# Query products of the second layer's attention: per batch inside the loop, or for four batches at once ahead of it

## Chip, cores and metric

One NeuronCore of a Trainium2 chip runs the whole program. The metric is the time of one execution on the device in microseconds (us), the median of several runs; smaller is better.

## The reference

Eight batches (B = 8) of 100 tokens (S) with 256 features (D) go through two transformer layers: attention and a mixture of experts, then latent attention and a gated network with 8-bit rounding. The change touches only the second layer's attention, which computes, for 16 heads:

```python
q_hk = (hidden_q @ Wq.T).reshape(Bv, Sv, H, K)
q_big = jnp.einsum('bshk,hkq->bshq', q_hk, w_kc_q)          # 192 features a head
q_big = _apply_rope(q_big, sin_q[...], cos_q[...])          # rotation by position
kv_r = _apply_rope(kv_c, sin_k[None], cos_k[None])          # 1444 keys of 64 features
q_r = jnp.einsum('bshq,hqr->bhsr', q_big, W_qr)
k_r = jnp.einsum('bld,hdr->bhlr', kv_r, W_kr)
scores = jnp.einsum('bhsr,bhlr->bhsl', q_r, k_r)
attn = jax.nn.softmax(scores, axis=-1)
ctx_c = jnp.einsum('bhsl,bld->bhsd', attn, kv_r)
```

`hidden_q` is the normalised output of the first layer, so no query can be made before the experts of the first layer have finished for that batch. The kernel has folded the weights beforehand: `wqb` and `wqt` hold Wq times w_kc_q (the first 128 and the last 64 of the 192 features of every head), `amat` holds W_qr times W_kr, so that a head's query ends as 64 "latent" numbers which meet the rotated keys directly.

## The kernel before

**Stages.** The first layer's attention and the folding of weights fill the first 140 us of the trace, the shared expert and the routed experts run until about 255 us. Then comes a stretch that this text calls the front (255.3 to 306.1 us), and then the loop over the second layer (306.1 to about 880 us), and a short end.

**The loop.** It runs over 8 batches with 48 slots each, or over 16 units `u` (half a batch: 8 heads, 24 slots; units 2b and 2b+1 are batch b). One slot is one `scores` (two products of a key tile with 400 query columns, a main part `qh` with `khl` and a remainder part `ql` with `kh1`, L1197) and one exponential on ACT (L1674) into one of eight buffers `pt`. Each slot from 1 to 21 of a unit also has one `max_chunk` of the next unit (L1177, 482 keys), reduced on DVE (`reduce_max`, L1976): the row maxima have to be known before the unit's own scores. After slots 7, 15 and 23 stand the `values` products of four tile pairs (L1209), so a unit has three phases of eight slots. POOL adds the exponentials up (`add_weights`, L614) and rotates the keys of the batch after next (L594 to L597). Between these, at fixed slots, stand the transposes of the next keys (`turn_keys`, L1158), the output product (L1232) and the gated network of the batch before. All engines work through orders that are written out by hand; they meet at semaphores only.

**The queries.** For unit u + 2, the loop of unit u makes: `q_big` (L1116 and L1121) with 100 columns (one batch's tokens) against the weights of each head, in the slots QB_AT = 1, 3, 5 of the first two phases; `rope` on DVE (L1943, L1947), which multiplies by cosine and sine into `xyz`; `q_latent` (L1143), after slot 23, ahead of the third values products; `keep_q` on ACT (L1592), which rounds to the fast 32-bit form `qh`; and `low_q` on DVE (L1957), which puts the rounding remainder into `ql`. Units 14 and 15 have no such work, since no unit u + 2 is left. The queries of units 0 and 1 are made in the front.

**The front.** The PE transposes batch 0's keys, makes the eight `shared_out` products of the first layer (L1008), transposes the normalised input `xn3` of batch 0 and 1 (`turn_x3`, L1098), the q work of units 0 and 1, all 21 maximum chunks of unit 0, and six transposes of the gated network's weights (`turn_ternary`, L1085). DVE finishes the first layer's output per batch (`second_residual` L1918, `third_input` L1923 to L1927) and normalises it (`norm_x3`, L1933); POOL fetches the experts' rows (`xn<-ys_scratch`, L689) and does the inverse roots (L636).

A float32 product of one tile is two passes in the trace, each an instruction of its own; a product in the fast form (`qh`, `ql`, `khl`) is one. The SP engine issues nearly all transfers in one hand-written order; `place_max` (L512) moves the row maxima into the last row of `ql`, and the first scores of a unit wait for it.

## Time and profile before

| what | value |
|---|---|
| median of 3 runs | 905.37 us (898.53 to 906.08) |
| span of the profiled execution, first to last instruction | 903.0 us (the page gives no other time for it) |
| busy share PE, DVE, ACT, POOL | 92%, 65%, 44%, 50% |
| front, 255.3 to 306.1 us: PE busy | 41.95 of 50.8 us |
| a middle unit pair, units 12 and 13 | 37.1 and 35.8 us |

The span is the sum that stages are taken from; the median of the runs lies 2.4 us above it. Busy shares are averages over stages: PE is busy for 36.21 of the 37.1 us of unit 12, and less in the front. "PEclk" is the clock that TensorE was granted: 1.00 is 2.4 GHz, 0.50 is 1.2 GHz.

### The profile page before, as it was taken

The numbers are of one execution on the slowest core, as the hardware profiler recorded it, in microseconds if no ns is written. First come the engines' busy times: TensorE is split into PE (matmuls) and PEld (weight loads), VectorE is DVE, ScalarE is ACT, GpSimd is POOL, SyncE is SP. The second block draws the span as 40 slices with busy tenths as digits, with TensorE's granted clock in tenths as the row PEclk, the third lists the DMA queues.
The fourth block names the chain that finished last, engine by engine and source line by source line (L and its number), as shares of the span: only waits on it lengthen the run. The fifth ranks groups of instructions, "written<-read, shape, count | busy, mean of one in ns | idle before, by whom it ended". The sixth has DMA issues, their size and how long they took to land.

```text
span 903.0 us, 15604 instructions
## 1 busy us (share of the span) xinstructions
PE 826.4 (92%) x5844; PEld 606.6 (67%) x5844; DVE 585.3 (65%) x1133; ACT 397.2 (44%) x883; POOL 453.2 (50%) x465
## 2 busy tenths in 40 slices
PE   4998879999998799999999999999999999999883
PEld 3566656788887667677667677676767766765442
DVE  3437864213358675677878778778787787786545
ACT  2248852222231454544544454454354454444441
POOL 3000002800041187768776876776776776567630
PEclk9979996999999899999999999999999999999986
DMA  9532022789810100000000100000000000000000
GB/s 212 187 123 89 2 67 79 261 299 317 299 46 10 35 1 12 18 10 10 19 10 1 31 10 2 10 26 7 10 23 10 10 6 10 2 16 10 2 13 11
DMA packets 42168, 52.28 MB, mean 58 GB/s; under 512 B 12230, under 2 KB 35704, under 8 KB 41836
## 3 DMA queue, kind: packets, MB, share of 16 engines
q1 hardware_dynamic: 41068, 49.63, 17.5%
q0 software_dynamic: 1024, 1.64, 0.6%
q8 instruction: 47, 0.77, 0.3%
q14 instruction: 29, 0.24, 0.1%
HBM read 45.80 MB, written 5.36 MB: 57 GB/s over the span
## 4 chain that ended last, share of the span: by engine, by line
PE 68%; DVE 13%; ACT 7%; DMA 5%; issue 5%; SPq 1%; POOL 0%; POOLq 0%; ACTq 0%; DVEq 0%
PE ps L1197 14%; PE ps L1209 10%; PE ps L1177 7%; PE ps L1116 6%; PE ps L1121 3%; PE ps L1232 3%; DMA xs<-xs_scratch 3%; PE ps L1042 3%; PE ps L994 3%; PE ps L1143 3%; ACT sm L1465 2%; PE ps L1055 2%; DVE xyz L1947 2%; DVE xyz L1943 1%; PE ps L893 1%
## 5 line engine op out<-in xcount | busy, mean ns | idle before, releaser
L614 POOL TENSOR_TENSOR acc<-acc,pt 120x800 f32<-120x800 f32 (+1 forms) x157 | 299.1, 1905 | 94.4 <-ACT pt L1674 61.4
L1674 ACT ACTIVATE pt<-ps 120x400 f32<-120x400 f32 (+1 forms) x384 | 190.1, 505 | 222.5 <-PE ps L1197 211.6
L1976 DVE TENSOR_REDUCE nm<-ps 128x1 f32<-128x482 f32 (+1 forms) x336 | 213.7, 655 | 100.3 <-PE ps L1177 98.1
L1197 PE MATMUL ps<-qh,khl 128*120 128x400 f32 (+1 forms) x384 | 157.9, 411 | 11.1 <-ACT pt L1674 8.3
L1209 PE MATMUL ps<-pt,kv 120*64 120x400 f32 (+1 forms) x768 | 143.8, 510 | 0.0
L1177 PE MATMUL ps<-khl,qh 128*128 128x482 f32 (+1 forms) x336 | 131.6, 393 | 5.3 <-DVE nm L1976 4.6
L1197 PE MATMUL ps<-ql,kh 65*120 65x400 f32 (+1 forms) x384 | 134.3, 350 | 0.0
L1197 PEld LDWEIGHTS ps<-qh,khl 128*120 128x120 f32 (+1 forms) x384 | 70.9, 185 | 58.6 <-issue 32.4
L1209 PEld LDWEIGHTS ps<-pt,kv 120*64 120x64 f32 (+1 forms) x768 | 51.9, 138 | 65.8 <-issue 55.8
L636 POOL TENSOR_TENSOR rstd<-veps,mhalf 100x1 f32<-100x1 f32 (+2 forms) x20 | 13.4, 670 | 158.1 <-DVE veps L1808 114.6
L1197 PEld LDWEIGHTS ps<-ql,kh 65*120 65x120 f32 (+1 forms) x384 | 71.3, 186 | 5.1
L1116 PEld LDWEIGHTS ps<-x3T,wqb 128*128 128x128 f32 x512 | 68.3, 195 | 3.1 <-issue 0.7
L614 POOL TENSOR_TENSOR acc<-pt,pt 121x800 f32<-121x800 f32 x16 | 30.6, 1910 | 77.0 <-ACT pt L1674 77.0
L1177 PEld LDWEIGHTS ps<-khl,qh 128*128 128x128 f32 (+1 forms) x336 | 60.1, 179 | 12.6 <-DVE nm L1976 8.9
L1116 PE MATMUL ps<-x3T,wqb 128*128 128x100 f32 x512 | 67.3, 275 | 0.7 <-ACT x3T L1429 0.5
L1042 PE MATMUL ps<-xsT,egu 128*128 128x128 f32 x448 | 52.6, 276 | 1.0 <-DVE hs L1900 0.6
L1042 PEld LDWEIGHTS ps<-xsT,egu 128*128 128x128 f32 x448 | 51.9, 192 | 1.8 <-ACT xsT L1429 1.3
L1592 ACT ACTIVATE qh<-ps 64x400 fp32r<-64x400 f32 x64 | 31.9, 499 | 46.6 <-PE ps L1143 46.1
L689 POOL DMA_INDIRECT xn<-ys_scratch,slot x8 | 8.5, 1067 | 78.2 <-DMA ys_scratch<-ysb 76.2
L1947 DVE TENSOR_TENSOR xyz<-ps,ropeq 64x200 f32<-64x200 f32 x128 | 46.2, 361 | 1.3
L1908 DVE TENSOR_TENSOR hT<-sg,ps 128x512 f32<-128x512 f32 x14 | 9.6, 686 | 48.2 <-PE ps L1042 48.2
L1232 PE MATMUL ps<-bmat,ct 128*100 128x256 f32 x128 | 33.5, 385 | 6.4 <-DVE ct L1997 5.8
(277 smaller groups left out, 1246.0 us busy)
## 6 DMA issues: line engine op xcount, KB each, us to landing
egu<-_L_ffn_gate_up_proj_dram SPq DMA_DIRECT2D x14, 1024.0 KB, 6.0
edn<-in_L_ffn_down_proj_dram SPq DMA_DIRECT2D x14, 512.0 KB, 7.1
spread<-inv_scratch SPq DMA_DIRECT2D x30, 100.0 KB, 2.7
craw<-in_ctx_dram SPq DMA_DIRECT2D x8, 360.0 KB
wo_n<-in_L_xattn_Wo_dram SPq DMA_DIRECT2D x1, 2048.0 KB, 10.5
wq_n<-in_L_xattn_Wq_dram SPq DMA_DIRECT2D x1, 2048.0 KB, 8.0
xs_scratch<-zero SPq DMA_DIRECT2D x1, 1792.0 KB, 9.9
xs<-xs_scratch SPq DMA_DIRECT2D x14, 128.0 KB, 6.1
```

What stands on the lines that cost most here:

```text
L614: nc.gpsimd.tensor_tensor(total[r, :, :], before[r, :, :], pt[j % PT_BUF][r, :, :], ALU.add).then_inc(p_added, 1)
L994: last = mm(ps[:, 2 * (k % 2) + a, 0:HT], sgu[:, c, a, 128 * m:128 * m + 128], xnT[:, c, HT * n:HT * n + HT], start=c == 0, stop=c == DC - 1)
L1042: last = mm(ps[:, 2 * (t % 2) + a, TR * m:TR * m + TR], egu[t % EBUF][:, c, FI * a + 128 * m:FI * a + 128 * m + 128], xsT[t % 2][:, c, :], ...
L1116: mm(ps[:, q_bank(u, a), S * part:S * part + S], wqb[:, c, h, 0:128], x3T[:, c, :], start=c == 0, stop=c == DC - 1)
L1177: mm(ps[0:w, 3 + m % 2, 0:MN], qh[u % 2][:, 128 * i:128 * i + w], khl[b % 2][:, MSTART[n]:MSTART[n] + MN], start=True, stop=True).then_inc ...
L1197: last = mm(ps[0:key_rows(t), k % 2, 0:HT], lhs[:, keys], rhs[:, HT * a:HT * a + HT], start=first, stop=not first)
L1209: last = mm(ps[CD * a:CD * a + CD, 2, 0:HT], kv[b % KV_BUF][r, t, :], pt[j % PT_BUF][r, a, :], start=t == 0, stop=t == KT - 1)
L1232: last = mm(ps[0:S, 6, 0:D], ct[:, S * i:S * i + S], bmat[:, i, :], start=i == 0, stop=i == GH - 1)
L1592: last = nc.scalar.activation(qh[u % 2][p:p + CD, HT * a:HT * a + HT], ps[CD * a:CD * a + CD, 5, 0:HT], ACT.Copy)
L1674: nc.scalar.activation(pt[j % PT_BUF][0:rows, k % 2, :], ps[0:rows, k % 2, 0:HT], ACT.Exp).then_inc(p_ready, 1)
L1947: last = tt(o[CD * j:CD * j + CD, 2, e:HG:2, :], ps[CD * e:CD * e + CD, bank + 1, 0:HT // 2].rearrange("p (i q) -> p i q", i=HG // 2), rop ...
L1976: nc.vector.tensor_reduce(nm3[0:w, i, n:n + 1], ps[0:w, 3 + m % 2, 0:MN], AX.X, ALU.max).then_inc(m_reduced, 1)
```

## The change

All queries are made before the loop, and no longer for one batch but for four batches side by side, so that the columns of a product grow from 100 to 400 (HT). The work is cut into eight quads `n`: `quad(n)` gives the half of the batches g, the half of the heads p and a pair of heads e; a quad makes four heads of four batches. Per quad:

- PE: `q_tail` twice (the last 64 features of two heads, 2 products), `q_main` four times (one head's first 128 features, 2 products), and `q_latent` of the quad before (12 products of 400 columns), which stands behind the two tails.
- DVE: four `rope`s of two multiplications each (was: six per `rope`), two `low_q`. ACT: four pairs of copies of tails into `tail2` (`keep_tail`) and two `keep_q`. POOL: four multiplications of tails by the rotation table (`rope_tail`).
- SP: `store_q`, four transfers of 64 x 4 x 200 numbers (205 KB each) into the DRAM tensor `q_scratch`.

For each unit of the loop `load_q` brings the queries back with three transfers of 64 x 800 numbers (205 KB each); `qh` and `ql` get a third buffer (QBUF = 3). The maximum chunks of unit 0 stand in quads 4, 5 and 6 (MAX_IN), the six weight transposes in quads 0, 2 and 3, the transposes of the inputs of batches 4 to 7 in quads 1 and 2. The loop loses `q_big`, `rope`, `q_latent`, `keep_q`, `low_q`, `turn_x3` and `norm_x3`; some waits that went with them change. Units 14 and 15 keep their instructions.

```diff
+HB = B // 2
+QUADS = 2 * NU // HB
+QBUF = 3
+MAIN_BANK, TAIL_BANK, LATENT_BANK = (0, 1), (6, 7), (2, 5)
+TERNARY_IN, X3_IN, MAX_IN = (0, 0, 2, 2, 3, 3), (1, 1, 2, 2), (4, 5, 6)
...
+        def store_q(sp, n):
+
+            g, p, e = quad(n)
+            sp.wait_ge(q_hi, 2 * n + 2)
+            sp.wait_ge(q_lo, 2 * n + 2)
+            heads = q_dram.rearrange("(g b p) l d (a e n) -> g p l a e d b n", g=2, b=HB, p=PAIRS, a=2, e=2)
+            for l, src in enumerate((qhi[e], qlo[e])):
+                for a in range(2):
+                    sp.dma_start(heads[g, p, l, a, e],
+                                 src[CD * a:CD * a + CD, :, :, :].rearrange("d b i s -> d b (i s)").bitcast(F32)).then_inc(q_stored[e], 16)
+
+        def load_q(sp, u):
+
+            n = 2 * PAIRS * (u // PAIRS // HB) + 2 * (u % PAIRS)
+            for e in range(2):
+                sp.wait_ge(q_stored[e], 64 * (n // 2 + 1))
+            if u == QBUF - 1:
+                sp.wait_ge(latent_done, 2 * QUADS)
+            elif u >= QBUF:
+                sp.wait_ge(s_done, LANE * (u - QBUF + 1))
...
-            place_max(sp, 0)
+            for n in range(4):
+                store_q(sp, n)
+            load_q(sp, 0)
+            load_q(sp, 1)
...
+            store_q(sp, 4)
+            store_q(sp, 5)
+            place_max(sp, 0)
+            store_q(sp, 6)
+            store_q(sp, 7)
             for u in range(NU):
                 b = u // PAIRS
+                if u + 2 < NU:
+                    load_q(sp, u + 2)
...
+            for e in range(2):
+                pool.wait_ge(q_stored[e], 64 * QUADS // 2)
             pool.wait_ge(fq_turned, 6)
...
+            def q_main(n, a, i):
+
+                g, p, e = quad(n)
+                m = 4 * n + 2 * a + i
+                if m >= 2:
+                    pe.wait_ge(rope_done, m - 1)
+                h = 2 * HG * p + HG * a + 2 * e + i
+                for c in range(DC):
+                    last = mm(ps[:, MAIN_BANK[i], 0:HT], wqb[:, c, h, 0:128], x3T[:, c, HT * g:HT * g + HT],
+                              start=c == 0, stop=c == DC - 1)
+                last.then_inc(main_done, 1)
...
                 if c == 0:
-                    pe.wait_ge(q_hi, u + 1)
+                    pe.wait_ge(ld_q[u % QBUF], 48 * (u // QBUF + 1))
...
+            for n in range(QUADS):
+                q_tail(n, 0)
+                q_tail(n, 1)
+                if n:
+                    q_latent(n - 1)
+                for a in range(2):
+                    for i in range(2):
+                        q_main(n, a, i)
+                        if n in MAX_IN:
+                            for c in range(MC):
+                                if c // 7 == MAX_IN.index(n) and c % 7 // 2 == 2 * a + i:
+                                    max_chunk(0, c)
...
-                    if u + 2 < NU and f < 2 and x in QB_AT:
-                        for part in range(2):
-                            q_big(u + 2, f, 2 * QB_AT.index(x) + part)
...
+            def rope(n, a, i):
+
+                m = 4 * n + 2 * a + i
+                dve.wait_ge(main_done, m + 1)
+                if n:
+                    dve.wait_ge(latent_done, 2 * n)
                 for j in range(2):
+                    last = tt(xy[a][i][:, j, :].rearrange("p (b q) -> p b q", b=HB),
+                              ps[:, MAIN_BANK[i], 0:HT].rearrange("p (b q) -> p b q", b=HB),
+                              ropeq[:, j, :].unsqueeze(1).to_broadcast([128, HB, S]), ALU.mult)
                 last.then_inc(rope_done, 1)
```

PE of the kernel before, in a first phase of unit 0 in the loop (x3T is the transposed input, wqb and wqt are the query weights, qh with khl is a score or a maximum chunk):

```order
516 L1197 MATMUL ps<-ql_198,kh_188 120x400
517 L1177 MATMUL ps<-khl_187,qh_197 128x482 [waits m_reduced]
518 L1158 MATMUL ps<-ident,kv_104 64x120 [waits k_kept,kv_ready]
519 L1158 MATMUL ps<-ident,kv_104 64x120 x3
520 L1197 MATMUL ps<-qh_196,khl_187 120x400 [waits p_ready]
521 L1197 MATMUL ps<-ql_198,kh_188 120x400
522 L1177 MATMUL ps<-khl_187,qh_197 128x482 [waits m_reduced]
523 L1116 MATMUL ps<-x3T,wqb 128x100 x4
524 L1197 MATMUL ps<-qh_196,khl_187 120x400 [waits p_ready]
```

PE of the changed kernel at the same place, in the first phase of the loop:

```order
611 L1283 MATMUL ps<-qh_202,khl_193 121x400 [waits p_ready]
612 L1283 MATMUL ps<-ql_203,kh_194 121x400
613 L1263 MATMUL ps<-khl_193,qh_204 128x482 [waits m_reduced]
614 L1242 MATMUL ps<-ident,kv_104 64x121 [waits q_lo,kv_ready]
615 L1242 MATMUL ps<-ident,kv_104 64x121 x3
616 L1283 MATMUL ps<-qh_202,khl_193 121x400 [waits p_ready]
617 L1283 MATMUL ps<-ql_203,kh_194 121x400
618 L1263 MATMUL ps<-khl_193,qh_204 128x482 [waits m_reduced]
```

Between the maximum chunk and the next score nothing of the queries is left.

PE of the changed kernel in quad 4, ahead of the loop (zt are rotated tails, xy rotated main features):

```order
492 L1226 MATMUL ps<-zt_232,amat 64x400
493 L1226 MATMUL ps<-zt_237,amat 64x400
494 L1209 MATMUL ps<-x3T,wqb 128x400 [waits rope_done]
495 L1209 MATMUL ps<-x3T,wqb 128x400
496 L1263 MATMUL ps<-khl_193,qh_202 128x482 [waits fq_kept,k_kept,ld_q0]
497 L1263 MATMUL ps<-khl_193,qh_202 128x482 [waits fq_kept]
498 L1209 MATMUL ps<-x3T,wqb 128x400 [waits rope_done]
499 L1209 MATMUL ps<-x3T,wqb 128x400
500 L1263 MATMUL ps<-khl_193,qh_202 128x482 [waits m_reduced] x2
```

The latent products of quad 3 end at 493; the first maximum chunk of unit 0 stands one head's main product behind them, and now waits for a transfer (ld_q0).

SP of the changed kernel at that time:

```order
150 L555 DMA q_scratch<-qhi_130 64x4x200 [waits q_lo,q_hi]
151 L555 DMA q_scratch<-qhi_130 64x4x200
152 L555 DMA q_scratch<-qlo_131 64x4x200 x2
153 L568 DMA qh_202<-q_scratch 64x800 [waits q_stored1,q_stored0]
154 L568 DMA qh_202<-q_scratch 64x800
155 L569 DMA ql_203<-q_scratch 64x800
```

The load of unit 0's queries stands behind the four stores of quad 3, which wait for the remainders (q_lo) of quad 3's latent products.

SP of the kernel before, at the end of the front:

```order
140 L468 DMA ys_scratch<-ysb_163 128x256 [waits ys_kept]
141 L512 DMA ql_198<-nmr_194 1x6x128 [waits m_kept]
142 L512 DMA ql_198<-nmr_194 1x16x2
143 L568 DMA lnw_b<-in_L_ffn_ln_weight_dram 100x1024 [waits fq_turned]
144 L480 DMA craw_105<-in_ctx_dram 120x768 [waits kv_ready]
```

Nothing stood between the experts' last store and the row maxima; now 32 stores and six loads do.

## Rows read from the trace of the kernel before

**Rows 1.** The page: busy time by engine, and the clock in 40 slices.
```profile
PE 826.4 (92%) x5844; PEld 606.6 (67%) x5844; DVE 585.3 (65%) x1133; ACT 397.2 (44%) x883; POOL 453.2 (50%) x465
...
PEclk9979996999999899999999999999999999999986
```
**Rows 2.** Busy time by stretch: front, cold start, units 0, 1, 12, 13, 14.
```profile
core 0: us, PE busy (x) PEld busy (x) DVE busy (x) ACT busy (x) POOL busy (x), PEclk, DMA share, GB/s
255.30:306.10 50.80, 41.95 (x344) 32.98 (x343) 36.53 (x83) 15.63 (x26) 12.41 (x13) 1.00 0.08 23
306.10:312.00 5.90, 5.87 (x21) 5.61 (x21) 2.84 (x7) 1.85 (x4) 0.00 (x0) 0.50 0.41 124
306.10:342.20 36.10, 35.38 (x226) 26.24 (x226) 24.43 (x50) 17.29 (x35) 25.84 (x23) 0.91 0.07 21
342.20:373.70 31.50, 31.48 (x223) 22.99 (x221) 20.52 (x40) 15.27 (x32) 24.90 (x22) 1.00 0.06 20
738.10:775.20 37.10, 36.21 (x249) 26.73 (x247) 28.74 (x62) 18.89 (x39) 22.07 (x15) 1.00 0.02 7
775.20:811.00 35.80, 35.05 (x247) 24.79 (x245) 27.62 (x47) 16.77 (x34) 21.48 (x12) 1.00 0.04 10
811.00:841.50 30.50, 28.93 (x141) 17.59 (x139) 21.09 (x43) 13.86 (x29) 19.67 (x12) 1.00 0.03 8
```
**Rows 3.** PE in order of time, unit 12: start, us, engine, line, operation.
```profile
739.19 1.03 PE L1116 MATMUL ps<-x3T,wqb 128*128 128x100 f32 x8
740.00 0.42 PE L1197 MATMUL ps<-qh,khl 128*121 128x400 f32 x1
...
742.73 0.58 PE L1158 MATMUL ps<-ident,kv 121*64 121x121 f32 x4
743.08 0.42 PE L1197 MATMUL ps<-qh,khl 128*121 128x400 f32 x1
```
**Rows 4.** PE in order of time, end of unit 12.
```profile
770.28 2.28 PE L1143 MATMUL ps<-xyz,amat 128*64 128x100 f32 x48
772.39 2.86 PE L1209 MATMUL ps<-pt,kv 120*64 120x400 f32 x16
775.18 0.45 PE L1197 MATMUL ps<-qh,khl 128*121 128x400 f32 x1
```
**Rows 5.** Groups by line: name, forms, count, busy us, mean ns, idle before.
```profile
L614 POOL TENSOR_TENSOR acc<-acc,pt 120x800 f32<-120x800 f32 (+1 forms) x157 | 299.1, 1905 | 94.4 <-ACT pt L1674 61.4 <-issue 17.0 <-POOL kv L597 8.6
L1976 DVE TENSOR_REDUCE nm<-ps 128x1 f32<-128x482 f32 (+1 forms) x336 | 213.7, 655 | 100.3 <-PE ps L1177 98.1
L1943 DVE TENSOR_TENSOR xyz<-ps,ropeq 128x400 f32<-128x400 f32 x64 | 33.4, 562 | 0.9 <-PE ps L1121 0.7
L1592 ACT ACTIVATE qh<-ps 64x400 fp32r<-64x400 f32 x64 | 31.9, 499 | 46.6 <-PE ps L1143 46.1
```
**Rows 6.** DVE in order of time, from unit 12 into unit 13.
```profile
769.94 0.41 DVE L2001 TENSOR_TENSOR x_sb<-x_sb,ps 100x256 f32<-100x256 f32 x1
...
776.47 1.15 DVE L1957 TENSOR_TENSOR ql<-ps,qh 64x400 fp32r<-64x400 f32 x2
```
**Rows 7.** Busy time of a stretch of the shared expert: PE only has 400-column passes.
```profile
156.00:169.50 13.50, 13.50 (x41) 7.60 (x40) 2.86 (x5) 2.59 (x6) 11.59 (x25) 1.00 0.98 356
```
**Rows 8.** PE in order of time, front.
```profile
271.18 1.89 PE L1008 MATMUL ps<-sdn,hs 128*100 128x256 f32 x8
```
**Rows 9.** SP's issues in order of time, unit 2.
```profile
384.91 1.18 SPq L489 DMA_DIRECT2D inv<-sums  x2
387.58 0.33 SPq L492 DMA_DIRECT2D inv_scratch<-inv  x1
388.94 1.13 SPq L499 DMA_DIRECT2D spread<-inv_scratch  x2
```
**Rows 10.** The page: DMA issues, KB each, us from issue to landing.
```profile
spread<-inv_scratch SPq DMA_DIRECT2D x30, 100.0 KB, 2.7
...
ys_scratch<-ysb SPq DMA_DIRECT2D x14, 128.0 KB, 6.1
```
**Rows 11.** PE in order of time, start of the loop.
```profile
306.13 0.66 PE L1197 MATMUL ps<-qh,khl 128*121 128x400 f32 x1 [2.34 <-DMA ql<-nmr]
```

More of the change, by code:

```diff
@@ L270, in build @@
         assert cursor[0] <= after_qb
+        cursor[0] = after_keys
+        xn3 = [place(f"xn3_{i}", [S, D]) for i in range(2)]
+        qhi = [place("qhi0", [128, HB, 2, S], F32R)]
+        qlo = [place("qlo0", [128, HB, 2, S], F32R)]
+        assert cursor[0] <= after_qb
+        cursor[0] = after_qb
+        qhi += [place("qhi1", [128, HB, 2, S], F32R)]
+        qlo += [place("qlo1", [128, HB, 2, S], F32R)]
+        assert cursor[0] <= after_fw
         cursor[0] = after_qb
@@ L1652, in _ @@
                 keep_keys(0, j)
[L1653 to L1662 removed]
+            for b in range(HB):
+                keep_x3(b)
+            for n in range(QUADS):
+                keep_tail(n, 0)
+                keep_tail(n, 1)
+                if n:
+                    keep_q(n - 1, 0)
+                    keep_q(n - 1, 1)
+                for t in range(6):
+                    if TERNARY_IN[t] == n and n < 2:
+                        keep_ternary(t)
+                for b in range(HB, B):
+                    if X3_IN[b - HB] == n:
+                        keep_x3(b)
+                for t in range(6):
+                    if TERNARY_IN[t] == n and n >= 2:
+                        keep_ternary(t)
+                if n == MAX_IN[-1]:
+                    keep_max(0)
+            keep_q(QUADS - 1, 0)
+            keep_q(QUADS - 1, 1)
             for b in range(B):
@@ L1696, in _ @@
                         keep_max(u + 1)
-                    if u + 2 < NU and at == LANE - 1:
-                        keep_q(u + 2)
             def last_silu(half):
@@ L1952, in low_q @@
-            def low_q(u):
-                dve.wait_ge(q_hi, u + 1)
-                for a in range(2):
-                    cols = slice(HT * a, HT * a + HT)
-                    last = tt(ql[u % 2][0:CD, cols], ps[CD * a:CD * a + CD, 5, 0:HT],
-                              qh[u % 2][CD * a:CD * a + CD, cols].bitcast(F32), ALU.subtract)
-                last.then_inc(q_lo, 1)
+                dve.wait_ge(rstd_ready, AFTER_3 + b + 1)
+                if b >= 2:
+                    dve.wait_ge(x3_turned, b - 1)
```

401 lines of the change are left out of this document (194 added, 207 removed).

## The prediction

> **What bounds the kernel now.** I read the page first [rows 1]: PE is busy for 92% of the span, at 2.4 GHz in nearly every slice, and no other engine for more than 65%. That is an average, so the stages come next, as stretches [rows 2]. In the loop, unit 12 lasts 37.1 us with PE busy for 36.21, unit 13 lasts 35.8 with 35.05: PE sets the pace, and DVE (28.74), POOL and ACT have room. In the front PE works 41.95 of 50.8 us. The first 5.9 us of the loop run at half clock. The most telling row is unit 14: it has no query work (no unit 16 follows), lasts 30.5 us, and PE stands idle for 1.6 of them. So query work costs time in the loop, and without it PE is no longer quite alone at the limit. Then I read single pieces in order of time, for what one piece costs on PE from the start of one instruction to the start of the next; "busy" and mean durations would overstate it, as passes overlap.
>
> **What the loop loses.** Eight passes of q_big take 0.81 us (739.19 to 740.00) [rows 3]; a unit has six such pieces: 4.9. The 48 passes of q_latent take 2.1 us (770.28 to 772.39) [rows 4]. Together 7.0 us a unit, for the 14 units 0 to 13.
>
> Not all of it comes back, because what was beside it has lost its cover:
> - Even units. Unit 14 is the template: 30.5 us [rows 2]. It lacks three key transposes, 0.35 us each (742.73 to 743.08) [rows 3], which the others keep. With them and a little for ACT's copies of the keys I take 31.9 us, against 37.1: 5.2 won of 7.0. The missing part is pacing: with no q_big between them, slots follow each other at PE's 0.6 us, but each has a reduction of 0.655 us on DVE [rows 5], and each maximum chunk waits for the second last reduction.
> - Odd units. From 769.94 to 776.47 DVE is occupied with the residual, the normalisation and the rounding of the batch before [rows 6]; the values products (775.18 less 772.39, 2.8 us) and the latent products (2.1 us) have covered that [rows 4]. Now 2.1 us of cover go, the third maximum chunk of the next unit waits, and I count 1.2 us of the 7.0 as given back: 5.8 won.
> - Six pairs (units 2 to 13): 6 x 11.0 = 66 us.
> - Units 0 and 1 [rows 2]: 36.1 less 7.0, less 2.9 for the half-clock start (5.9 us of work at half rate), which I expect to vanish, as PE comes out of dense products; and 31.5 less 7.0. Plus 0.5 for pacing that makes 51.2. POOL, however, needs 11 additions of 1.905 us [rows 5] and some 6 us of key rotation a unit, 27 us, 54 for two, and begins only when quad 7's stores have landed, about 7 us into the loop. The sums of unit 1 are wanted some 7.5 us into unit 2, so PE waits about 3 us: 54. From 67.6: 13 won.
>
> Loop: 79 us won. The ends are 101 us (14 x 7.0 + 2.9, nothing given back) and 70 us (a further 0.7 us lost a unit).
>
> **What the front gains.** First the price of a 400-column pass: in a stretch of the shared expert with nothing else on PE, 40 to 41 passes start in 13.5 us [rows 7], 0.336 us each. The latent products write half the output columns each and run in pairs as the values products do: 16 passes of 400 columns in 2.8 us (772.39 to 775.18) [rows 4], 0.174 each. So a quad has 2 tails of 4 passes (2.7 us), 4 mains of 4 passes (5.4) and 24 latent passes (4.2): 12.3 us, and eight quads 98 us. All 16 units of the old way cost 16 x 7.0 = 112 us. Larger products save PE just 14 us, since a 100-column pass is already cheap in place (0.10 us) and four times the columns cost 3.3 times that. Everything else about this change is where the time lies and what waits.
>
> A rule points elsewhere. The Trainium skill, "TensorE: Matmul & The Clock Gate", section "Back-to-back issue gap", gives N / 2.4 + 2.5 ns for an isolated product at full clock, 0.169 us for 400 columns; the row of float32 passes shows twice that [rows 7]. By that rule of the Trainium skill the quads' 288 pass times would take 49 us instead of 97, and the sum would come out 48 us lower.
>
> The front in order:
> 1. Until the first tail product. The four remaining shared_out products (1.89 us each [rows 8]) alternate on DVE with residual, normalisation and PE's transpose, some 3.4 us a round from 265: first tail at 278.7 us. POOL has two memsets ahead of the first rotation, so `rope` starts near 284.
> 2. Quad 0 without latent products, with two weight transposes: done at 289. Within a quad DVE does not delay PE: a rope is two multiplications of 0.56 us [rows 5], 1.1 against 1.34 for a main product. ACT's tail copies (0.5 us each [rows 5], 8 a quad) and POOL's four multiplications (between a half and one addition of 800 columns [rows 5], at most 7.6 us a quad) also fit into 12.3.
> 3. Quads 1 to 3 with four input and four weight transposes: 3 x 12.3 + 4 = 41: 330.
> 4. Quad 4: tails and the latent products of quad 3 end at 337. Now the first maximum chunk of unit 0 is one main product (1.3 us) away, and its load stands on SP behind the four stores of quad 3, which wait for ACT and DVE to split quad 3's latent products (about 1.4 us). SP spends 0.59 us on an issue (1.18 for two, 1.13 for two) [rows 9]; seven issues are 4.1, and a load of 100 KB lands 2.7 us after its issue [rows 10]. The last of the three loads is issued 5 us after the latent end and lands at about 8, so PE stands for some 7 us. What hides it otherwise is nothing: the chunk blocks every product behind it. Bounds: 4 us (issues at half price) and 14 (a store of 128 KB needs 6.1 us under load [rows 10], and the loads queue behind 820 KB).
> 5. Behind a pause of 2.34 us PE ran 5.9 us at half clock at the start of the loop [rows 2, 11]. After 7 us I expect the same, 2.4 us lost. Bounds: 0 and 3.
> 6. Quads 4 to 6 carry seven reductions of 0.655 us each beside four ropes of 1.1 (9.0 us of DVE [rows 5]) against 6.8 us of PE in the same stretch; part of it runs on under the tails. 1.4 us lost a quad, and 2.5 behind quad 6, where the transpose of the maxima waits for the last reduction. Quad 7 ends with 1.4 us of wait for its last rope, since no tails follow.
>
> Sum: 337 + 1.3 + 6.8 (stall) + 2.4 (half clock) + 6.9 (three mains, seven chunks at 0.2 us, 1.4 of DVE) = 354.4 for quad 4; quads 5 and 6 15.1 each (12.3 + 1.4 + 1.4), and 2.7 behind them; quad 7 12.3, and its last wait and latent products 5.6: the loop starts at about 405 instead of 306 us, 99 us later. Bounds: 85 (no stall, no DVE pacing) and 112.
>
> The Trainium skill, "DMA: Bandwidth & Descriptors", section "Anatomy of one DMA", gives 2.0 us plus bytes over 436 GB/s. That rule makes the seven transfers (1.43 MB) 5.3 us, and the stall would shrink only if SP's issue time were nil.
>
> **The sum.** 903.0 + 99 - 79 = 923 us against the profiled span. The three runs reach from 4.5 below the span to 3.1 above it, so the median gives no firm offset, and I take 922.
>
> **Rivals.**
> - *The loop gives everything back (ends faster).* Its place is slots 24 to 31 and 0 to 7 of the loop. If DVE's chains are not the limit there, each unit wins 7.0: 101 us, less POOL's 3. With the front at 99 that is 904; if the load also arrives in time (9 less), it is 895, and with the DVE wait behind quad 6 gone too, 893. It counts as faster from 7.0 a unit on. For it: PE is 97% busy and DVE 77% in unit 12 [rows 2]. Against it: unit 14, where PE idles for 1.6 us with less to do. Time 893 to 904.
> - *The load is in time, the loop paced as I say.* If stores and load overlap PE fully, 9 us less: 914. For it speaks that units 0's and 1's queries are long stored by then; against it SP's order.
> - *Transfers bind every quad.* A quad stores 820 KB in four issues. `keep_q` needs the stores of two quads ago, so it decides once the queue moves less than 820 KB in 12.3 us, 67 GB/s. At 55 GB/s (15 us) six quads lose 2.6 each, 16 us: 939. Against it: 356 GB/s moved in one stretch [rows 7].
> - *POOL rules the loop.* With 27 us a unit against 31 it does not; at full pace it would only cap an upside at 27 a unit.
> - *The small products were free and the loop loses nothing.* Then 1000 us; unit 14 excludes it.
>
> **Chances.** A measurement of this kernel can tell about 1% (9 us) from no change. Forecast with its own spread 0.62 (909 to 933), of which some 0.10 falls within 1% of before; load in time 0.14, most of it within 1%; loop gives all back 0.10, half within 1% and half faster; transfers bind 0.13, slower; the rate of the Trainium skill's page on TensorE 0.01, 874 us, faster. That is faster 0.06, within 1% 0.27, slower 0.67. The range 904 to 938 takes in the late-transfer case nearly whole and the in-time case, and leaves the fastest out.
>
> **What would show it.** Right: the loop starts near 405 us; passes in the quads start 0.336 us apart; one wait of 5 to 9 us at L1263 for the load of qh near 338 us, with half clock behind it; units 2 to 13 at 61 to 63 us a pair; unit 14 unchanged at 30.5. Wrong: quads longer than 13 us with PE waiting at L1226 for DVE, ACT or POOL; no wait at the first maximum chunk; pairs under 60 us (then the loop gave back less than I took) or over 65, with POOL's additions back to back.

## The result: 928.1 us, 2.7% slower

| | before | after |
|---|---|---|
| median | 905.7 us (898.5 to 906.5, 4 runs) | 928.1 us (924.3 to 933.7, 4 runs) |
| ratio | 1 | 1.0267, 95% interval 1.0211 to 1.0324 |
| profiled execution: span | 903.0 | 931.8 (its time was 933.7) |
| first keys transposed (end of the first layer) | 255.5 | 263.1 |
| front, from there to the first score of the loop | 50.6 | 148.1 (+97.5) |
| first score of the loop to the end | 596.9 | 520.6 (-76.3) |

I had predicted 922 (904 to 938), a front longer by 99 and a loop shorter by 79. The 7.6 us by which the first keys come later lie in code that the change doesn't touch. Over all traces of this study, of both kernels, this point lies anywhere between 252.8 and 263.1 us, about as wide as the run times of one kernel spread (898.5 to 906.5 before, 924.3 to 933.7 after). Hence the sections of the traces, front and loop, are the sharper measure, and I use them beside the ratios: 647.5 us before, 668.7 after. Each is read from a single execution, though. The comparison leaves out runs over 1.5% above the fastest of their kernel; where one run came out very short (888.5 in b_port, 883.7 in a_keys_dve) this bends the ratio of the runs that are left, and there I go by the medians of all runs and by sections.

The page of the changed kernel, busy time and clock, answers to [rows 1]: PE is still the busiest, but its share fell from 92% to 89%.

```profile
PE 830.6 (89%) x4692; PEld 534.7 (57%) x4692; DVE 538.4 (58%) x989; ACT 404.1 (43%) x899; POOL 487.7 (52%) x502
...
PEclk9869997999999998999998999999999999999996
```

The stretches that answer to [rows 2] (us, then busy PE, PEld, DVE, ACT, POOL, granted clock, DMA share, GB/s): front, first 5.9 us of the loop, units 0, 1, 12, 13 and 14.

```profile
263.10:411.20 148.10, 129.99 (x547) 67.58 (x545) 70.70 (x152) 52.91 (x103) 49.11 (x51) 0.97 0.21 57
411.20:417.10 5.90, 5.89 (x33) 4.42 (x33) 4.37 (x7) 4.58 (x10) 0.00 (x0) 1.00 0.51 134
411.20:437.27 26.07, 25.24 (x132) 15.46 (x130) 15.80 (x26) 15.58 (x32) 17.84 (x16) 1.00 0.27 70
437.27:462.28 25.01, 24.73 (x123) 14.53 (x123) 15.11 (x24) 12.98 (x27) 23.47 (x23) 1.00 0.12 33
779.69:810.77 31.08, 29.54 (x152) 18.81 (x150) 23.66 (x45) 16.79 (x35) 21.97 (x17) 1.00 0.09 27
810.77:842.92 32.15, 29.90 (x148) 18.11 (x148) 22.13 (x36) 14.71 (x30) 23.35 (x13) 0.95 0.11 29
842.92:872.21 29.29, 28.44 (x140) 17.62 (x138) 21.14 (x42) 13.85 (x29) 19.67 (x13) 1.00 0.03 8
```

Three things stand out. The loop starts at a granted clock of 1.00 (0.50 before). The even unit 12 is 6.0 us shorter. The odd unit 13, which was shorter than the even one before (35.8 against 37.1), is now longer than it: 32.15 us, PE idle for 2.2 of them, and its clock is 0.95.

The stall in quad 4, PE in order of time:

```profile
343.19 1.61 PE L1209 MATMUL ps<-x3T,wqb 128*128 128x400 f32 x4
353.25 1.17 PE L1263 MATMUL ps<-khl,qh 128*128 128x482 f32 x2 [8.45 <-DMA ql<-q_scratch]
354.22 2.87 PE L1209 MATMUL ps<-x3T,wqb 128*128 128x400 f32 x4
```

and SP's issues beside it:

```profile
344.52 1.23 SPq L555 DMA_DIRECT2D q_scratch<-qhi  x2
345.79 1.33 SPq L555 DMA_DIRECT2D q_scratch<-qlo  x2
347.54 1.16 SPq L568 DMA_DIRECT2D qh<-q_scratch  x2
348.75 0.60 SPq L569 DMA_DIRECT2D ql<-q_scratch  x1
```

Seven issues of some 0.6 us, four stores and three loads, follow the latent products of quad 3; the third load is issued at 348.75 and has landed when PE goes on at 353.25. Behind the wait the same four passes span 2.87 us instead of 1.61, and the granted clock is 0.50 for 4 us:

```profile
353.25:357.20 3.95, 3.95 (x7) 2.49 (x8) 1.30 (x3) 0.00 (x0) 0.00 (x0) 0.50 0.62 164
```

That is the wait that I had placed there, at 8.45 us instead of 6.8.

Where PE waits in the loop, units 0 to 13, changed kernel (us in total, times, longest):

```profile
PE ps L1263 <- DVE nm L2061: 15.4, 12, 2.9
PE ps L1283 <- ACT pt L1769: 8.9, 14, 0.8
PE ps L1304 <- POOL acc L680: 0.6, 1, 0.6
```

The same view of the kernel before:

```profile
PE ps L1232 <- DVE ct L1997: 5.8, 7, 0.8
PE ps L1197 <- ACT pt L1674: 4.0, 7, 0.7
PE ps L1197 <- DMA ql<-nmr: 2.3, 1, 2.3
PE ps L1177 <- DVE nm L1976: 2.1, 5, 0.5
```

The wait for DVE at the maximum chunks has grown sevenfold, and 11.5 of the 15.4 us lie in the first phases of the odd units 3 to 13, one wait in each. These phases last (unit 3, 5, ... 13) 14.7, 12.7, 12.75, 11.4, 11.4, 12.4 us, where the first phase before (11.1 to 12.15) less its three pieces of `q_big` (2.4) would be 8.6 to 9.7.

### The profile page after: what moved, and what is told of

The parts are those of the page before. It is cut to its first block, busy times and chain, and to the rows that moved or that the text cites. A ratio compares the mean times of both kernels' runs of the same rounds, so it can differ in the third digit from the quotient of the medians.

```text
span 931.8 us, 13330 instructions
## 1 busy us (share of the span) xinstructions
PE 830.6 (89%) x4692; PEld 534.7 (57%) x4692; DVE 538.4 (58%) x989; ACT 404.1 (43%) x899; POOL 487.7 (52%) x502
## 4 chain that ended last, share of the span: by engine, by line
PE 59%; DVE 15%; POOL 8%; ACT 7%; DMA 5%; issue 5%; SPq 1%; POOLq 0%; DVEq 0%; ACTq 0%
PE ps L1283 9%; PE ps L1295 8%; POOL acc L680 6%; PE ps L1263 5%; PE ps L1125 4%; PE ps L1209 4%; PE ps L1226 4%; DVE nm L2061 3%; PE ps L1077 3%; DMA xs<-xs_scratch 2%; PE ps L1316 2%; ACT sm L1542 2%; PE ps L1138 2%; PE ps L1197 2%; DVE sg L2129 1%
## 5 line engine op out<-in xcount | busy, mean ns | idle before, releaser
L2061 DVE TENSOR_REDUCE nm<-ps 128x1 f32<-128x482 f32 (+1 forms) x336 | 211.1, 652 | 115.8 <-PE ps L1263 113.8
L1263 PE MATMUL ps<-khl,qh 128*128 128x482 f32 (+1 forms) x336 | 138.1, 414 | 25.5 <-DVE nm L2061 16.1
L702 POOL TENSOR_TENSOR rstd<-veps,mhalf 100x1 f32<-100x1 f32 (+1 forms) x25 | 15.6, 624 | 167.6 <-DVE veps L1899 120.4
L1263 PEld LDWEIGHTS ps<-khl,qh 128*128 128x128 f32 (+1 forms) x336 | 61.7, 184 | 46.8 <-DVE nm L2061 28.8
L775 POOL TENSOR_TENSOR zt<-tail,ropeq 128x400 f32<-128x400 f32 x32 | 33.3, 1045 | 76.9 <-ACT tail L1506 75.9
L1209 PE MATMUL ps<-x3T,wqb 128*128 128x400 f32 x128 | 48.9, 522 | 1.2 <-DVE xy L2033 1.2
L1506 ACT ACTIVATE tail<-ps 64x400 f32<-64x400 f32 x64 | 31.9, 499 | 37.5 <-PE ps L1197 32.8
L680 POOL TENSOR_TENSOR acc<-pt,pt 121x800 f32<-121x800 f32 x16 | 30.7, 1921 | 22.8 <-DMA q_scratch<-qlo 11.2
L2033 DVE TENSOR_TENSOR xy<-ps,ropeq 128x400 f32<-128x400 f32 x64 | 33.7, 568 | 10.7 <-PE ps L1209 8.3
L2043 DVE TENSOR_TENSOR qlo<-ps,qhi 128x400 fp32r<-128x400 f32 x16 | 9.2, 575 | 49.5 <-ACT qhi L1676 49.5
```

What stands on the lines that cost most here:

```text
L680: nc.gpsimd.tensor_tensor(total[r, :, :], before[r, :, :], pt[j % PT_BUF][r, :, :], ALU.add).then_inc(p_added, 1)
L775: nc.gpsimd.tensor_tensor(zt[m % 8][:, :].rearrange("p (b q) -> p b q", b=HB), tail2[i][:, :].rearrange("p (b q) -> p b q", b=HB), ropeq[: ...
L1209: last = mm(ps[:, MAIN_BANK[i], 0:HT], wqb[:, c, h, 0:128], x3T[:, c, HT * g:HT * g + HT], start=c == 0, stop=c == DC - 1)
L1263: mm(ps[0:w, 3 + m % 2, 0:MN], qh[u % QBUF][:, 128 * i:128 * i + w], khl[b % 2][:, MSTART[n]:MSTART[n] + MN], start=True, stop=True).then_ ...
L1506: return nc.scalar.activation(dst, src, ACT.Copy, **more)
L2033: last = tt(xy[a][i][:, j, :].rearrange("p (b q) -> p b q", b=HB), ps[:, MAIN_BANK[i], 0:HT].rearrange("p (b q) -> p b q", b=HB), ropeq[:, ...
```

## The experiments

Two questions: does the stall cost what it seems to, and what holds the odd units? Names with a_ start from the changed kernel, names with b_ from the one before. The sections are read from each trace; the fronts of kernels whose instructions are the same up to there differ by 2.7 us, since the first tail product starts 21.7 us after the first keys in some traces and 24.3 to 24.5 in others; so fronts are compared from the first tail product on.

| run | front | loop to end | sum | ratio to before (95%) |
|---|---|---|---|---|
| before | 50.6 | 596.9 | 647.5 | 1 |
| after | 148.1 | 520.6 | 668.7 | 1.0267 (1.0211 to 1.0324) |
| a_load_early | 140.4 | 520.5 | 660.9 | 1.0141 (1.0086 to 1.0196) |
| b_no_queries | 50.6 | 526.5 | 577.1 | 0.9226 (0.9187 to 0.9266) |
| a_half_adds | 150.5 | 499.8 | 650.3 | 1.0072 (1.0033 to 1.0110) |
| b_half_adds | 50.6 | 592.5 | 643.1 | 0.9980 (0.9928 to 1.0032) |
| a_x4_late | 147.9 | 524.9 | 672.8 | 1.0262 (1.0199 to 1.0326) |
| b_x4_late | 50.6 | 597.6 | 648.2 | 1.0015 (0.9963 to 1.0067) |
| a_spread | 135.4 | 520.3 | 655.7 | 1.0119 (1.0045 to 1.0193) |
| a_best | 138.2 | 523.4 | 661.6 | 1.0202 (1.0130 to 1.0274) |
| a_port | 147.7 | 505.1 | 652.8 | 1.0043 (1.0011 to 1.0076) |
| a_spread_port | 135.4 | 501.9 | 637.3 | 0.9949 (0.9918 to 0.9980) |
| b_port | 50.6 | 593.6 | 644.2 | 0.9873 (0.9817 to 0.9930); medians 900.3 against 902.9 |
| a_keys_dve | 135.4 | 502.7 | 638.1 | 0.9876 (0.9799 to 0.9953); medians 897.5 against 900.9 |

### The load earlier: a_load_early

```diff
-            for n in range(4):
-                store_q(sp, n)
-            load_q(sp, 0)
+            store_q(sp, 0)
+            store_q(sp, 1)
+            load_q(sp, 0)
+            store_q(sp, 2)
+            store_q(sp, 3)
             load_q(sp, 1)
```

> The changed kernel, with the loads of unit 0's and unit 1's queries issued as soon as their quads are stored (load of unit 0 behind the stores of quad 1, load of unit 1 behind those of quad 3). Theory A (SP's order makes the stall, the pause makes the half clock): the wait of 8.45 us at the first maximum chunk goes, and the half-clock stretch behind it too; quad 4, from its first tail to that of quad 5, falls from 25.3 to 14.9 us like quads 5 and 6, and the whole kernel by 10 to 11 us, to 917. Theory B (stores and loads together are too slow for the front, whatever their order): the wait moves or shrinks to 4 us or more, and the kernel gains under 5 us. If only the wait goes and the half clock stays, 8.5.

Theory A. The tails of quads 4 and 5 in this run:

```profile
329.49 2.91 PE L1199 MATMUL ps<-x3T,wqt 128*128 128x400 f32 x8
344.38 2.85 PE L1199 MATMUL ps<-x3T,wqt 128*128 128x400 f32 x8
```

Quad 4, from one row to the other, takes 14.9 us instead of 25.25, so the stall with its slow stretch cost 10.4: 8.45 of waiting and 1.9 of half clock. The ratio to before fell from 1.0267 to 1.0141, some 11 us. It was the order of one queue and not the transfers themselves.

### What the loop can give: b_no_queries

Units 2 to 15 of the kernel before reuse the first two units' queries; nothing is made in their place.

> The kernel before, with the query work of units 2 to 15 left out of the loop on PE, DVE and ACT (q_big, rope, q_latent, keep_q, low_q, and the transposes and normalisations of inputs 2 to 7); these units reuse the queries of units 0 and 1, so the output is not that of the reference. It prices what the loop can give back at most. My prediction's terms: 79 us (70 to 101) gained by the loop; here POOL starts on time, so 82: 905 - 82 = 823. Rival (the loop gives back all 7.0 us a unit): 98 to 101 us, 805. Rival (the odd units' waits in the changed kernel come from missing cover on DVE, not from POOL's late start): units 3, 5, 7 and 9 take 31.5 us or more here too and the gain is 75 or less. If POOL's late start makes them: odd units 30.4 to 31.2 from the beginning.

The loop section is 70.4 us shorter, where I expected 82. Two causes. Its first unit gained only 0.8 us, since the first phase now runs at a granted clock of 0.62 with waits (17.5 us). And the odd units are long without POOL's late start too: unit 3 takes 29.8 us, but units 5 and 9 take 32.35, with 12.6 us in their first phase at a clock of 0.86, like unit 5 of the changed kernel. That is the rival of the missing cover. So POOL's late start cannot be the whole cause; only unit 3 (first phase 9.7 here, 14.7 in the changed kernel) seems to hang on it.

### POOL's additions halved: a_half_adds, b_half_adds

```diff
-            nc.gpsimd.tensor_tensor(total[r, :, :], before[r, :, :], pt[j % PT_BUF][r, :, :], ALU.add).then_inc(p_added, 1)
+            w = 2 if t == 1 else 1
+            nc.gpsimd.tensor_tensor(total[r, 0:w, :], before[r, 0:w, :], pt[j % PT_BUF][r, 0:w, :], ALU.add).then_inc(p_added, 1)
```

> The changed kernel with POOL's additions halved from the second of a unit on (400 of 800 columns a row, 10 of 11 additions), so the sums of half the heads are wrong. Theory P (POOL, which starts 7 us late and has 27 us of work a unit, is behind until unit 5, holds up the inverse root for the rounding chain, and so the maximum chunks of odd units): units 3, 5, 7, 9 fall from 33.5, 33.2, 32.5, 31.1 to about 31, the whole by 5 to 8 us, to 920 to 923. Theory D (DVE's chain itself is too long for the slots): they stay within 0.5 us, and the whole within 2 us of the changed kernel.

> Control: the same halved additions in the kernel before. There POOL idles 2 to 3 us in stretches of a unit, so both theories expect nothing: within 2 us of 905. A gain of more than 3 us would mean that POOL's additions hold the loop up in the kernel before too (or contend with DVE), and then the gain of the halved additions in the changed kernel would say nothing of its late start.

The changed kernel's loop gained 20.8 us, three times what theory P expected, the kernel before 4.4. The 4.4 us are more than the 3 that I had set for the control (by the medians of the runs it is 2.4): the additions cost the kernel before something as well, so the gain is no measure of POOL's late start. Every odd unit fell, those of the middle too. The first phase of unit 5 with whole additions, that of unit 9, and then that of unit 5 with halved ones (us, busy PE, PEld, DVE, ACT, POOL, clock, DMA share, GB/s):

```profile
557.82:570.50 12.68, 10.92 (x53) 6.93 (x54) 7.87 (x13) 5.12 (x12) 11.14 (x13) 0.87 0.17 49
685.66:697.08 11.42, 9.57 (x54) 5.62 (x54) 7.84 (x13) 5.03 (x12) 10.83 (x12) 1.00 0.20 54
```

```profile
545.26:554.95 9.69, 9.56 (x53) 5.62 (x54) 6.14 (x12) 5.01 (x12) 8.17 (x12) 1.00 0.25 64
```

PE's idle 1.8 us are gone, and so is DVE's extra 1.7 us of "busy" time, though DVE's instructions are the same. That was the hint. The two engines side by side at the start of unit 5, changed kernel:

```profile
555.83 0.61 POOL L702 TENSOR_TENSOR rstd<-veps,mhalf 100x1 f32<-100x1 f32 x1 [2.85 <-DVE veps L2090]
556.41 3.94 POOL L680 TENSOR_TENSOR acc<-acc,pt 120x800 f32<-120x800 f32 x2
...
557.24 1.20 DVE L2102 TENSOR_SCALAR xn<-xn,qsc 100x256 f32<-100x256 f32 x1
...
559.11 1.40 DVE L2110 TENSOR_SCALAR xq<-xn 100x256 bf16<-100x256 f32 x1
...
561.99 0.49 PE L1263 MATMUL ps<-khl,qh 128*128 128x482 f32 x1 [1.74 <-DVE nm L2061]
```

POOL waits for the variance; meanwhile the additions of slots 21 and 23 pile up and run back to back from 556.41, one until about 558.4 (half of the 3.94 us) and one until 560.35. DVE's scaling of xn ends at 558.44 and that of xq at 560.51, each within 0.2 us of the end of an addition. With halved additions the same two take 0.354 and 0.484 us in the mean, with whole ones 1.10 and 1.24. DVE stands still while POOL adds; the trace counts it as busy.

The Trainium skill, "SBUF — State Buffer", section "Who interferes with whom", says that VectorE and GpSimd share one pair of ports, which an instruction holds to its end, that `tensor_scalar` can contend for it (in the modes that use both ports), and so do operations with both inputs in SBUF, while `tensor_reduce` on this chip never does. The trace agrees, though no row names the mode in which the scalings run: the maxima take 0.655 us before, 0.652 after and 0.652 with halved additions, but the division `ct<-ctu,spread`, with both inputs in SBUF, shows this in the groups of before, of after and of a_half_adds:

```profile
L1997 DVE TENSOR_TENSOR ct<-ctu,spread 128x400 f32<-128x400 f32 x15 | 9.8, 654 | 2.9 <-DMA spread<-inv_scratch 2.5
```

```profile
L2082 DVE TENSOR_TENSOR ct<-ctu,spread 128x400 f32<-128x400 f32 x15 | 20.1, 1339 | 7.5 <-DMA spread<-inv_scratch 7.3
```

```profile
L2083 DVE TENSOR_TENSOR ct<-ctu,spread 128x400 f32<-128x400 f32 x15 | 9.3, 621 | 6.7 <-DMA spread<-inv_scratch 6.5
```

The change doubled it without touching it, and halved additions take that back: the same instruction now falls where POOL is adding.

### The root later: a_x4_late, b_x4_late

```diff
-    OUT_FROM, RESIDUAL_SLOT, QX_SLOT, X4_SLOT = 17, 21, 23, 19
+    OUT_FROM, RESIDUAL_SLOT, QX_SLOT, X4_SLOT = 17, 21, 23, 23
```

> The changed kernel with POOL's inverse root for the rounding chain placed behind the addition of slot 23 instead of slot 19 (X4_SLOT = 23); nothing else. Theory Q (while POOL waits for the variance, the additions of slots 21 and 23 pile up, and run back to back right behind the root; DVE's two large scalings of the chain, 0.35 and 0.48 us with halved additions, 1.20 and 1.38 with whole ones, stand still until POOL's addition ends): with the additions done ahead of the root both scalings fall to 0.35 to 0.6 us, the first phase of units 5 to 13 from 12.7 or 11.4 to 10 to 11 us, and the whole kernel by 6 to 9 us, to about 0.992 to 0.994 of the changed kernel. Theory R (POOL is simply behind, 27 us of work a unit, and what counts is how late the root comes): the root comes up to 1.9 us later and the kernel gains nothing or loses up to 5 us. Unit 3, where POOL is still behind from its late start, should keep its 14.7 us by both.

> Control: the same X4_SLOT = 23 in the kernel before. There the latent products cover the chain; the halved additions shortened an odd unit by only 0.6 us. Both theories: within 3 us of the kernel before, at most 4 us faster.

Half a miss: theory Q is right on the scalings, theory R on the time. Both scalings fell (0.353 and 0.470 us), but the odd first phases of units 5 to 13 stayed at 11.2 to 13.95 us, that of unit 3 grew to 18.3, and the loop to 524.9. DVE and PE at the start of unit 11:

```profile
743.11 0.21 DVE L2099 TENSOR_SCALAR qsc<-qsc,rstd 100x1 f32<-100x1 f32 x1 [2.04 <-POOL rstd L702]
...
743.81 0.35 DVE L2102 TENSOR_SCALAR xn<-xn,qsc 100x256 f32<-100x256 f32 x1
...
746.34 0.77 PE L1263 MATMUL ps<-khl,qh 128*128 128x482 f32 x1 [1.53 <-DVE nm L2061]
```

The root now comes 2.04 us late, behind the two additions. What the port no longer takes, the queue takes. An edit that takes away both was needed. The control did nothing, as expected.

### The front and POOL's start: a_spread, a_best

a_spread has the early loads, `c * 16 // MC == 4 * (n - 3) + 2 * a + i` for the place of a maximum chunk (quads 3 to 6), the weight transposes in quads 0 and 2, `turn_max(0)` behind the tails of quad 7, and two waits of POOL apart:

```diff
-            for e in range(2):
-                pool.wait_ge(q_stored[e], 64 * QUADS // 2)
+            pool.wait_ge(q_stored[0], 64 * QUADS // 2)
...
+                        if b == 0 and s == ROTATE_SLOT[0]:
+                            pool.wait_ge(q_stored[1], 64 * QUADS // 2)
```

> The changed kernel with three edits ahead of the loop: the early loads of a_load_early; the 21 maximum chunks of unit 0 spread over the 16 main products of quads 3 to 6 instead of 12 of quads 4 to 6, the weight transposes all in quads 0 and 2, and the transpose of the maxima behind the tails of quad 7; and POOL waits for the stores of the even quads only before its first addition, for those of the odd quads before its first key rotation. Against a_load_early: if DVE's seven reductions beside four ropes pace quads 4 to 6 (14.9 us against 12.9 of a quad without chunks), quads 3 to 6 take 13.0 to 13.6 us, the wait for the maxima (1.9 us) goes, and the front is 5 to 7 us shorter, less about 1 us for the moved transposes. POOL starts 4 to 5 us earlier, which takes 2 to 5 us from units 3 and 5. Sum 7 to 11 us: a ratio to the kernel before of 1.002 to 1.006. Rival (PE's own work, not DVE, fills the chunk quads): under 2 us from the front.

> a_spread and X4_SLOT = 23 together. If theory Q holds and the gains add, 6 to 9 us below a_spread: 0.993 to 0.999 of the kernel before. Unit 3 should gain too here, since POOL is less behind when its root comes. If theory R holds, the same as a_spread or slower.

The front: quads 3 to 6 take 14.3, 13.7, 13.7, 13.7 us, the chunk quads of a_load_early 14.9, 14.85, 16.9 (with the wait for the maxima). The moved transposes cost 2.3 in quad 2 and save 0.9 in quad 3, 1.4 where I had said 1. Behind the first tail the front is 113.7 us against 116.0: 2.3 won, not 5 to 7. The earlier start of POOL took 1.0 us from unit 3's first phase (14.7 to 13.7) and nothing measurable from the whole loop (520.3). So quads 3 to 6 gained 3.7 us beside the transposes, 1.9 of it the wait for the maxima; the other 1.8 I put down to DVE's pacing. The transposes take 1.4 of it back. a_best joined it with the late root, and that fails here too: with a ratio of 1.0202 it is slower than a_spread (1.0119), as theory R says.

### Neither queue nor port: a_port, b_port, a_spread_port

```diff
                     if b and s == X4_SLOT:
                         norm_x4(pool, power, b - 1)
+                        if b + 2 < B:
+                            rotate_keys(pool, step, b + 2, 2)
+                        pool.wait_ge(xq_ready, b)
...
-                    if b + 2 < B and s in ROTATE_SLOT:
+                    if b + 2 < B and s in ROTATE_SLOT and not (b and s == 23):
                         rotate_keys(pool, step, b + 2, ROTATE_SLOT.index(s))
```

> The changed kernel with one change of POOL's order for batches 1 to 7: the inverse root stays at slot 19, but behind it come the key rotation of slot 23 (four short multiplications and additions of 0.3 to 0.8 us) and a wait until the rounding chain has written xq, and only then the additions of slots 21 and 23. No work is added or left out. Theory Q (additions that run back to back behind the root hold DVE's two large scalings up, PE then waits 1.7 us, and at three or four units its clock falls): both scalings take under 0.6 us, the first phases of units 5 to 13 fall from 11.4 to 12.75 us to 9.7 to 10.3, PEclk 1.00 in all of them; unit 3 falls by 2 us or more from 14.7 (POOL is still behind there); from the first score to the end 505 to 509 us instead of 520.6, the ratio to the kernel before 1.009 to 1.015. Theory R (POOL's total work is the limit, and time that it stands idle for DVE is added to it): first phases as long as before or longer, or the sums (wait for the last addition) late by 1 to 3 us a unit, 518 to 530 us.

> a_spread with the same order of POOL. Sections of the trace, which leave out how late the first layer ends: front 135.4 us as in a_spread, first score to the end 505 to 508, together 641 to 643, against 647.5 of the kernel before: ratio 0.990 to 0.996. If theory R holds, 1.01 or more, no better than a_spread.

> Control: the same order of POOL in the kernel before. The scalings get shorter there too (1.10 and 1.24 us before), but the latent products cover the chain: the first phases of odd units fall by at most 0.6 us (12.15 to 11.5 or 11.6, as with halved additions), 0 to 4 us in all. If it gains 8 us or more, the additions cost the kernel before as much as the changed one, and the port says nothing about the change.

Theory Q: both scalings are short, every first phase is short at full clock, and the loop takes 505.1 us. It is better than theory Q's own figures in two places, the first phases (9.4 us, where 9.7 to 10.3 was said) and the ratio (1.0043, where 1.009 to 1.015 was said). POOL and DVE at the start of unit 5 in a_port, and its first phase as a stretch:

```profile
543.84 0.61 POOL L702 TENSOR_TENSOR rstd<-veps,mhalf 100x1 f32<-100x1 f32 x1 [2.72 <-DVE veps L2093]
...
546.69 4.29 POOL L680 TENSOR_TENSOR acc<-acc,pt 120x800 f32<-120x800 f32 x2 [0.73 <-DVE xq L2113]
...
545.25 0.35 DVE L2105 TENSOR_SCALAR xn<-xn,qsc 100x256 f32<-100x256 f32 x1
...
546.27 0.28 DVE L2113 TENSOR_SCALAR xq<-xn 100x256 bf16<-100x256 f32 x1
```

```profile
545.72:555.10 9.38, 9.32 (x55) 5.64 (x54) 5.74 (x12) 5.03 (x12) 8.22 (x6) 1.00 0.24 66
```

The first phases of units 5 to 13 take 9.4 us, unit 3's 10.0, all at a clock of 1.00; the odd units 28.8 to 29.95. The loop gained 15.5 us by 0.7 us of idling and an order, with no work less. (The key rotation moved as well; what that does by itself was not measured.) In the kernel before the same order is worth 3.3 us by sections (12.15 to 11.5 us a first phase) and 2.6 by medians: there the latent products had covered what the port takes. The ratio of b_port, 0.9873, would say more, but it hangs on the run of 888.5 us. The three edits of the front and this one together (a_spread_port, 897.8 us against 902.9, ratio 0.9949) beat the kernel before by half a per cent. Against the kernel before with the same order the sections say the same (637.3 against 644.2), but they are one trace each, and the medians, 897.8 and 900.3, are no further apart than such runs scatter; that this version is the faster one is not shown.

### What the even units give back: a_keys_dve

```diff
+                if b:
+                    nc.vector.tensor_copy(khl[b % 2][CD:128, k0:k0 + n], ps[0:CD, 5, 0:n])
                 tt(khl[b % 2][0:CD, k0:k0 + n], ps[0:CD, 5, 0:n], kh1[b % 2][0:CD, k0:k0 + n].bitcast(F32), ALU.subtract)
```

(and ACT's copy into khl left out from batch 1 on)

> a_spread_port, and for batches 1 to 7 one of ACT's two copies of each third of the transposed keys is made by DVE instead (21 copies of 64 x 480 numbers). In a_spread_port PE still waits in the loop 17 times, 10.3 us in all, for ACT's exponentials, in the first two phases of the even units, where ACT has both key copies between its exponentials. Theory K (these copies, not DVE's reductions, are what the even units give back: 31.1 us where 37.0 less 7.0 would be 30.0): the waits for ACT fall below 2 us in all, the even units from 31.1 to 29.9 to 30.3 us, the first score to the end from 501.9 to 493 to 496 us, and the ratio to the kernel before from 0.995 to 0.986 to 0.989. Theory D (my prediction's: the reductions pace the slots, 0.655 us against PE's 0.6): with 0.5 us more on DVE per key tile group the even units stay at 31.1 or grow by up to 0.5 us, and PE's waits move to DVE.

A miss for theory K. Theory D's numbers came true, but not by its mechanism, since the new wait is for a key copy and not for the reductions. An even unit of a_spread_port has two waits; ACT and PE in order of time:

```profile
682.25 1.07 ACT L1735 ACTIVATE hq<-h 100x1024 bf16<-100x1024 f32 x1
...
683.86 0.45 PE L1289 MATMUL ps<-qh,khl 128*121 128x400 f32 x1 [0.54 <-ACT pt L1775]
...
694.33 0.56 ACT L1512 ACTIVATE khl<-ps 64x480 fp32r<-64x480 f32 x1
...
695.47 0.44 PE L1289 MATMUL ps<-qh,khl 128*120 128x400 f32 x1 [0.69 <-ACT pt L1775]
```

The first stands behind ACT's square of the gated network and stayed. The second stood behind the key copies and went, but 0.72 us for DVE at the next key transposes came in its place:

```profile
699.37 0.57 PE L1248 MATMUL ps<-ident,kv 120*64 120x120 f32 x4 [0.72 <-DVE khl L2061]
```

since its copy (0.652 us) now runs in a row with the subtraction. Over the loop PE waits 6.5 us for ACT instead of 11.0, and 5.0 for `khl`. The even units 6 to 12 take 31.2 to 31.3 us, where a_spread_port has 31.0 to 31.1; sections and medians show no difference from a_spread_port. The ratio, 0.9876, lies in theory K's range, but it rests on three runs with the one of 883.7 us among them; the medians make it 0.996.

## Why the prediction was right, and where not

**Right: the sign, the size, and the front.** 928.1 measured, 922 predicted. The front grew by 97.5 instead of 99 us. Its terms: the stall 8.45 (6.8 said), its half clock 1.9 (2.4), DVE's pacing of the chunk quads 0.9 each (1.4; it is 14.85 less 12.55 and my 1.4 for seven chunks), the wait for the maxima 1.9 (2.5), quad 7 with its last rope and latents 18.1 (17.9), quads 1 to 3 with their transposes 40.65 (41). The wait stands where it was said to, and a_load_early showed its cause. It came out longer mainly because the last load took 4.5 us from issue to landing (348.75 to 353.25), where I had taken 2.7 from a smaller transfer. The fit of the Trainium skill, "DMA: Bandwidth & Descriptors", section "Anatomy of one DMA", that I had set beside it says nothing here as I used it: it is given for one transfer, and for those that GpSimd issues, while these seven are issued one after the other by SyncE. That PE gains little by larger products holds: a quad without chunks or transposes is 12.55 us, 0.25 more than my sum. The rate that I had set against it, that of the Trainium skill, "TensorE: Matmul & The Clock Gate", section "Back-to-back issue gap" (0.169 us for 400 columns, an estimate from its formula), is out: the 16 passes of a quad's main products start 0.347 us apart (5.55 us in all).

The closeness of the loop, 76.3 against 79, is luck: the next paragraphs add up errors of 13.9 us one way and 11.1 the other. Nor did all signs come true: of the six pairs of units 2 to 13 two took 61 to 63 us and four 63.2 to 64.4, and unit 14 did not stay at 30.5.

**Wrong: the odd units.** The step is "Odd units ... I count 1.2 us of the 7.0 as given back: 5.8 won". Measured over units 3 to 13 they won 3.5 us each (35.9 to 32.4), so 3.5 us were given back and not 1.2, 13.9 us more than I had said over the six units. The place was right, DVE's chain between 769.94 and 776.47 [rows 6], and so was the thought that it loses its cover; the size was wrong, and the prediction shows no working for it. Most of what is missing lies in the first phases of the odd units: PE stands idle there for 1.5 to 2.9 us each, 1.9 in the mean, and behind the wait the clock fell in four of the six (0.77, 0.87, 0.87, 0.86), which took about 2.8 us in unit 3 and 1.3 in the three others. The prediction had no term for the clock here.

Why the chain is so long I had not seen either. I read 6.5 us of "busy" DVE as work, but 1.7 of them are DVE standing still for POOL's additions, and they did so in the kernel before too:

```profile
771.88 3.92 POOL L614 TENSOR_TENSOR acc<-acc,pt 120x800 f32<-120x800 f32 x2
```

```profile
772.71 1.20 DVE L2017 TENSOR_SCALAR xn<-xn,qsc 100x256 f32<-100x256 f32 x1
...
774.58 1.37 DVE L2025 TENSOR_SCALAR xq<-xn 100x256 bf16<-100x256 f32 x1
```

The two scalings take 1.20 and 1.37 us, where 0.35 and 0.48 are enough beside shorter additions. So the hold is not made by the change; the change took the cover from it. Since the 6.5 us had the hold in them, it does not explain why 1.2 was too little, but it shows what the loss hangs on: remove the hold (a_port) and odd units win 6.6 of 7.0 (35.9 to 29.3).

**Wrong, but small: the even units.** They won 5.95, not 5.2. I had blamed DVE's reductions for pacing the slots (0.655 against 0.6). The rows show that PE waits for ACT instead, 0.5 and 0.7 us a unit; a_keys_dve shows that DVE stands close behind ACT, so that relieving one alone gives nothing. They had a gain that I did not see: before, PE waited 0.8 us for `ct` in each of them, and that wait is gone. Unit 14, my template, had that wait too (30.5 us before, 29.3 after). +4.5 in all.

**Units 0 and 1** won 16.5, not 13: the half clock at the loop's start went as expected, but POOL's late start cost PE only 0.6 us there, where I had put 3. It showed up one unit pair later, as 5 us more in the first phase of unit 3 than in b_no_queries. **Units 14 and 15** with the end, whose instructions did not change, won 3.1 us that I had not counted: 1.2 in unit 14 and 1.9 behind it, chiefly in the second phase of unit 15 (14.7 to 12.3 us), which other traces have anywhere between 10.6 and 14.7.

Together: 79 - 13.9 + 4.5 + 3.5 + 3.1 = 76.2, and the trace has 76.3.

**The rivals.** "POOL rules the loop" I had excluded by its sum, 27 us a unit against 31. The sum was right and the conclusion wrong: POOL's total is no limit (a_port keeps all of it), but when it works decides how long DVE takes. "The loop gives everything back" came true only with POOL's order mended: a_spread_port's loop is 95 us shorter than before, where I had put 98 for that case. "Transfers bind every quad" is out: quads without chunks keep to 12.55 us and their transposes, and no wait for a store shows but POOL's at the loop's start. "The load is in time" is a_load_early.

## What to carry to other kernels

When an engine's work is moved away, ask of what was beside it not only how long it is, but whether its time is its own: compare a group's mean duration with the shortest of its kind, and look at what VectorE's neighbour GpSimd does in the long ones. Work that piled up while GpSimd waited for VectorE was released exactly into VectorE's critical chain; there it paid to let the short work go first and the long work wait for the chain's end. Such a hold may have been there all along: it costs something once its cover is taken away. And a load that is needed early should not stand in a queue behind stores that wait for later results.
